# Cross-attention block on one core: layer-norm work moved within VectorE's attention step, and probability transposes that wait tile by tile

## What is computed

```python
xq = layer_norm(x, qn_w, qn_b)
ctx = layer_norm(context, cn_w, cn_b)
q = (xq @ q_w).reshape(B, N, H, D)
kv = (ctx @ kv_w).reshape(B, M, 2, H, D)
attn = jnp.einsum('bnhd,bmhd->bhnm', q, k) * scale
attn = jax.nn.softmax(jnp.where(xa_mask[:, None, :, :], neg, attn), axis=-1)
out = jnp.einsum('bhnm,bmhd->bnhd', attn, v).reshape(B, N, C) @ proj_w + proj_b
x = x + out
h = layer_norm(x, n2_w, n2_b)
return x + jax.nn.gelu(h @ fc1_w + fc1_b, approximate=False) @ fc2_w + fc2_b
```

## Time and profile before

| what | us |
|---|---|
| median of 3 runs | 1137.99 |
| lowest and highest run | 1137.99, 1138.52 |
| the profiled execution, span from first to last instruction | 1135.9 |
| TensorE busy | 1100.3 |
| VectorE busy | 606.5 |
| ScalarE busy | 404.4 |
| GpSimd busy | 234.7 |

### The profile page before, as it was taken

One profiled execution on the slowest core, in us unless ns is written; L12 is line 12 of the kernel. 1 busy time (PEld: TensorE's weight loads), 2 busy tenths in 40 slices (PEclk: granted clock), 3 DMA queues, 4 the chain that ended last, 5 costly groups with the idle time before them and its releaser, 6 DMA issues.

```text
span 1135.9 us, 16366 instructions
## 1 busy us (share of the span) xinstructions
PE 1100.3 (97%) x5849; PEld 941.0 (83%) x5849; DVE 606.5 (53%) x1154; ACT 404.4 (36%) x1158; POOL 234.7 (21%) x186
## 2 busy tenths in 40 slices
PE   4999999999999999999999999999999999999998
PEld 4789988999889888888888888888888888888887
DVE  7898999899999765632423322323333333232212
ACT  3456655566666744421211311221221131121110
POOL 2343444444554420100100100100110110010000
PEclk9999999999999999999999999999999999999999
DMA  7011111232111024202002002002001001100101
GB/s 245 8 35 58 38 38 47 65 93 65 39 57 39 29 91 145 71 19 74 1 1 75 1 2 74 1 1 74 1 1 64 13 1 38 38 1 1 38 1 38
DMA packets 40144, 48.76 MB, mean 43 GB/s; under 512 B 10965, under 2 KB 19197, under 8 KB 40087
## 3 DMA queue, kind: packets, MB, share of 16 engines
q1 hardware_dynamic: 37919, 43.74, 11.7%
q10 hardware_dynamic: 2168, 4.21, 1.0%
HBM read 30.54 MB, written 16.78 MB: 42 GB/s over the span
## 4 chain that ended last, share of the span: by engine, by line
PE 85%; DVE 5%; POOL 4%; issue 3%; ACT 2%; DMA 0%; ACTq 0%; POOLq 0%; DVEq 0%
PE bank L1304 31%; PE bank L1275 31%; PE bank L1144 7%; PE bank L1175 6%; POOL S L531 4%; PE bank L1125 4%; PE bank L1157 3%; ACT S L637 1%; PE bank L1186 1%; PE bank L1287 1%; DVE xhat L893 1%; DVE cx L773 1%; DVE esum L868 0%; PE bank L1135 0%; DVE S L828 0%
## 5 line engine op out<-in xcount | busy, mean ns | idle before, releaser
L1304 PE MATMUL bank<-w,gTh 128*128 128x512 f32 x1024 | 319.3, 393 | 0.0
L1045 DVE CAST gTh<-g 128x512 fp32r<-128x512 f32 x128 | 56.9, 444 | 442.9 <-ACT g L739 442.9
L739 ACT ACTIVATE g<-bank,cols 128x512 f32<-128x512 f32 x128 | 88.0, 688 | 471.6 <-PE bank L1275 470.1
L1304 PEld LDWEIGHTS bank<-w,gTh 128*128 128x128 f32 x1024 | 192.4, 188 | 42.7
L1304 PE MATMUL bank<-w,gTl 128*128 128x512 f32 x512 | 200.4, 391 | 0.0
L1275 PE MATMUL bank<-hT0h,w 128*128 128x512 f32 x512 | 162.2, 397 | 0.0
L1275 PE MATMUL bank<-hT1h,w 128*128 128x512 f32 x512 | 159.1, 392 | 0.1
L480 POOL TENSOR_TENSOR hrs<-hve,mhalf 128x1 f32<-128x1 f32 x32 | 17.6, 549 | 551.3 <-DVE hve L1019 551.3
L1304 PEld LDWEIGHTS bank<-w,gTl 128*128 128x128 f32 x512 | 96.1, 188 | 22.0
L1275 PEld LDWEIGHTS bank<-hT0h,w 128*128 128x128 f32 x512 | 94.7, 188 | 21.5
L1275 PEld LDWEIGHTS bank<-hT1h,w 128*128 128x128 f32 x512 | 95.1, 188 | 19.8 <-issue 0.5
(11 more groups left out here) (103 smaller groups left out, 1824.8 us busy)
## 6 DMA issues: line engine op xcount, KB each, us to landing
xr<-in_x SPq DMA_DIRECT2D x16, 512.0 KB, 3.5
x_scratch<-xr SPq DMA_DIRECT2D x16, 512.0 KB, 2.8
x<-x_scratch SPq DMA_DIRECT2D x8, 1024.0 KB, 5.6
out<-x SPq DMA_DIRECT2D x7, 1024.0 KB, 4.3
w1raw<-in_L_xattn_fc_w SPq DMA_DIRECT2D x16, 256.0 KB, 3.0
w2raw<-in_L_xattn_fc_w SPq DMA_DIRECT2D x16, 256.0 KB, 2.6
kvw<-in_L_xattn_kv_w ACTq DMA_DIRECT2D x2, 1024.0 KB, 11.1
qraw<-in_L_xattn_q_w ACTq DMA_DIRECT2D x1, 1024.0 KB, 11.6
```

The source lines that it names most:

```text
L739: act.activation(g[:, :], bF[j % 2][:, :], ACT.Gelu, bias=cols[:, F1B + j:F1B + j + 1]).then_inc(a_gelu.sem, 1)
L1045: dve.tensor_copy(gT[HI][j % 4][:, :], g[:, :]).then_inc(v_ghi.sem, 1)
L1304: mm = pe.matmul(bC[t][:, :], gT[d][j % 4][:, t * P:(t + 1) * P], w2[:, j, w, :], start=(j == 0 and i == 0), stop=(j == JT - 1 and i == 2))
```

## The change

In steps 0 to 15 (`prep` is None) VectorE executes `stats` between `masked(1, 2)` and `masked(1, 3)`, and not behind `prob_lo(3)`. It executes `variance` right behind `masked(1, 3)`, and not behind `av_lo(2)`. It executes `normed` behind `q_lo(0)`, ahead of `av_lo(1)`, and not behind `recip(0)`, ahead of `exp_sum`. GpSimd's `rstd` goes ahead of the subtraction, and stood behind it. TensorE waits for the scaling of tile 0 ahead of `prob_T1(0, 0)` and for that of tile 1 ahead of `prob_T1(0, 1)`; before, it waited for both ahead of `prob_T1(0, 0)`. No instruction that computes is added or removed, and the order in the preparation is as it was.

```diff
@@ GpSimd, step
+            def x_rstd():
+                n = k.plus(3)
+                v_veps.wait(pool, n, 0)
+                v_xhat.wait(pool, n.plus(-1), UT - 1)
+                power(rstd[:, :], veps[:, :], P).then_inc(p_rstd.sem, 1)
+
             if norm2 is not None:
                 h_rstd(static(0), norm2)
+            if norm and prep is None:
+                x_rstd()
             if scores:
                 n = k.plus(1)
                 v_max.wait(pool, n, 1)
...
-            if norm:
-                n = k.plus(3)
-                v_veps.wait(pool, n, 0)
-                v_xhat.wait(pool, n.plus(-1), UT - 1)
-                power(rstd[:, :], veps[:, :], P).then_inc(p_rstd.sem, 1)
+            if norm and prep is not None:
+                x_rstd()
@@ VectorE, step
             if scores:
                 masked(1, 2)
+            if norm and prep is None:
+                stats()
+                v_bn.wait(dve, n, UT - 1)
+            if scores:
                 masked(1, 3)
+            if norm and prep is None:
+                variance()
...
             if front:
                 q_lo(0)
+            if norm and prep is None:
+                normed()
...
-            if norm and prep is None:
-                stats()
-                v_bn.wait(dve, n, UT - 1)
             if back:
                 av_lo(2)
...
-            if norm and prep is None:
-                variance()
...
-            if norm and prep != "q":
+            if prep == "scores":
                 normed()
-            if prep == "scores":
                 values_lo(1)
@@ TensorE, prob_T1
-                if i == 0:
-                    p_prob.wait(pe, b, UT - 1)
+                if g_ == 0:
+                    p_prob.wait(pe, b, t)
```

## The result

| what | before | after |
|---|---|---|
| median of the runs, us | 1137.92 (17 runs) | 1140.09 (17 runs) |
| lowest and highest, us | 1137.13, 1138.52 | 1139.14, 1141.11 |
| span of the profiled execution, us | 1135.9 | 1138.5 |
| a loop step on TensorE, mean of steps 2 to 9, us | 23.32 | 23.43 |

The ratio is 1.002 with a 95% interval of 1.0013 to 1.0027. So the change costs about 2.2 us. That is 0.19%, right at the edge of what I had called no change. The range of 1134.5 to 1142 held it, and the direction of the small remainder is up. In all that follows, medians are of undisturbed executions; one execution, of experiment one, took 2829 us, nothing here shows why, and it is left out.

What follows compares the result with a forecast made beforehand. TensorE, busy 1100 of 1136 us, was taken to bound the kernel. A start stall of -1.40, `q(0)` +0.10 and mid-step wait +1.15 a step summed over all steps to 0.0, giving 1138.0 us, range 1134.5 to 1142.

Steps and rivals of the forecast that it cites:

- Part 1: At the step's start, TensorE's stall for GpSimd's scaling of tile 1 goes whole: 1.40 us a step.
- The new wait at `q(0)`: Near the step's start, `q(0)` waits for the second `x_lo`: 0.10 us a step, between 0 and 0.2.
- Part 2: Mid-step, early statistics and variance delay `prob_lo(2)` by 1.64 us; TensorE waits 1.15 us in each of 13 steps.
- Part 3: `normed` behind `q_lo(0)`: the pair costs 1.05 us on VectorE and TensorE loses 0, at most 0.3 a step.
- So it costs 0, with 0.05 us to spare: At `av(3)`: `prob_lo(3)` ends at 166.37 and TensorE wants it at 166.42, so no wait.
- my own sign: Prediction is wrong if `av(3)` waits for `PTl` by more than 0.1 us.
- The sum by step: Step 0 +1.15 us, steps 1 to 10 -0.15 each, 11 and 12 +0.51 each, 13 -0.6, others 0: together 0.0.
- the forecast: Whole kernel: 1138.0 us, within 0.2% of no change, a step of 23.2 to 23.3 us; chance 0.58.
- The slower one: At `av(3)`: `prob_lo(3)` is late, TensorE waits 0.25 to 0.3 us in each of 13 steps, 1141.5 us; chance 0.20.
- the change does nothing at the start: Rival: the stall at the step's start stays, +15 us, 1153 us; chance 0.02.
- the banks come free earlier: Faster rival, mid-step: the wait for `prob_lo(2)` costs 0.9 us, 13 times -0.25, 1134.8 us; chance 0.14.

Runs made afterwards that it cites:

- experiment one: Kernel before with only TensorE's wait split by tile (tile 0's scaling ahead of the first transposes, tile 1's ahead of the second): 1132.8 us, ratio 0.9956.
- nine: Changed kernel with TensorE's old wait, both scalings ahead of the first transposes: 1140.19 us, ratio 1.002.
- five: Kernel before with one edit, the normalisation right ahead of `recip(0)`, TensorE's old wait kept: 1123.3 us, ratio 0.9871.
- six: Kernel before with the normalisation ahead of `recip(0)`, plus the change's early `stats`, `variance` and `rstd`, old wait kept: 1137.64 us, ratio 1.000.
- four: Kernel before with two edits, the normalisation right ahead of `recip(0)` and TensorE's wait by tile: 1124.1 us, ratio 0.9876.
- two: Changed kernel with the normalisation put back behind `recip(0)`; early statistics, variance, `rstd` and wait by tile kept: 1147.56 us, ratio 1.0081.
- three: Changed kernel with the normalisation moved behind `prob_lo(3)`, all else as changed: 1138.12 us, ratio 0.9999.
- experiment eight: Changed kernel with the normalisation moved ahead of `q_lo(0)` instead of behind it: 1150.36 us, ratio 1.0112.

## Why the prediction was right, and where it was off

**The whole splits into three measured parts.** They come from kernels that differ in one of them, but for the wait by tile, which nine shows to be worth nothing in the changed kernel. The normalisation clear of GpSimd's scaling of tile 0: 1123.3 against 1137.9, -14.6 us (five). Statistics and variance ahead of `prob_lo(2)`: 1137.6 against 1123.3, +14.3 (six). The normalisation ahead of `prob_lo(3)` and not ahead of `recip(0)`: 1140.1 against 1137.6, +2.5 (with the old wait of TensorE on both sides, nine against six, 1140.2 against 1137.6). Together +2.2, which is the result. The wait by tile is worth 0 here (nine), and also in the fastest kernel (five against four: 0.8 us the other way, on two chips and with overlapping intervals of the ratios, so not resolved). It is worth 5 us only where the scaling of tile 1 is late (one).

**Part 1, the stall that goes: right.** I had 1.40 us a step. The timeline gives 1.32 at the first transposes and 1.38 one score later. One of my two reasons was that the pair's 3.02 us at the old place were mostly a wait for GpSimd; one swap shows it (five). The other, the wait for each tile, did nothing here (nine).

**The new wait at `q(0)`: right in kind, 0.18 and not 0.10.** I had left out that the first matmul after the wait takes 0.10 us longer (0.22 against 0.12). In part 2 I had counted some 0.1 for that as an estimate.

**Part 2, `prob_lo(2)` late: right.** I had 1.64 us of delay and 1.15 of wait; the traces have 1.65 and 1.10, and experiment six has 1.10 from medians. The rival in six, that the wait needs VectorE to be behind from elsewhere, is refuted: it is the same 0.63 in the profile's count in the changed kernel, in two, three and six.

**Part 3, the pair behind `q_lo(0)`: its price right, its consequence wrong.** I priced the pair at 1.05 us and it costs 1.03. (The 1.00 in it was the length of the merged row; to the next start an undisturbed pair takes 0.91, as in five, so the overlap with the subtraction cost 0.12 and not 0.05.) The failed step is the next one, "So it costs 0, with 0.05 us to spare". `prob_lo(3)` ends at 167.19, 0.03 ahead of the matmul's place at 167.22, as I had worked out, and TensorE is still 0.19 us late. The deadline that I used is the matmul's start. But the wait for `prob_lo(3)` also holds the weight load in front of that matmul, which goes 0.11 us ahead when nothing waits, and the load began 0.12 us after `prob_lo(3)`'s end. I had counted a hand-over and a late weight load in part 2 and neither here. By my own sign, a wait of `av(3)` by more than 0.1, this part was wrong: it is 0.19 late in starts, though the profile shows no bracket. Experiment three takes it away, and with it 2.0 us; this is most of the difference between the predicted 1138.0 and the measured 1140.1.

**The sum by step.** From the steps' starts in both traces: steps 2 to 9 cost 0.11 us more each where I had -0.15, so a step is 23.43 us and not the 23.2 to 23.3 of the forecast. Of the difference 0.19 is `av(3)`, 0.08 `q(0)`, and 0.05 that I took one step of 23.37 for all, while every other one took 23.28; 0.05 came back in part 2. Step 1 cost 0.16 more and step 10, which also holds work of the MLP block, 0.22 (23.96 against 23.74), where I had -0.15 for both. Together steps 1 to 10 took 1.3 us more and not 1.5 less. Steps 11 and 12 cost 0.3 each (I had 0.51), because the stall at their start was 0.9 in starts and not the 0.74 of the profile's count; for the same reason step 13 gained 0.97 (I had 0.64). Step 0 lost 1.26 (I had 1.15). The profiled execution after also has 0.4 us more in the preparation, whose order is unchanged. Its cause is open. Executions differ there by some of it: with the same order on VectorE, step 1 begins at 79.99 in experiment nine and at 80.23 in the changed kernel. The steps 11 to 13 came out 0.7 us better than I had them, and that hid part of the 2.8 us by which steps 1 to 10 came out worse. The time came 2.1 us above 1138.0, and the forecast's bounds were 2.3, so that it held was in part luck.

**The rivals.** The slower one named the right place, `prob_lo(3)` for `av(3)`, with "0.25 to 0.3 in each of 13 steps" and a threshold of 0.18 a step. The place and the size came true, 0.19 us. Its condition did not: the pair lost 0.12 us (1.03 to the next start, against 0.91 in experiment five) and not the whole 0.35. I gave it 0.20 and the forecast 0.58; with a room of 0.05 us against a mistake of 0.2 in the deadline, the two should have been even. That the change does nothing at the start and that the banks come free earlier are both refuted by the first timeline.

**The rule of the Trainium skill** ("SBUF — State Buffer", section "Who interferes with whom": whoever comes second stands still) fits three places. The `xhat` that met a GpSimd instruction ended 0.29 us after it in the kernel before (168.30 + 2.48, against 170.49), 0.28 after it in the changed kernel (165.08 + 0.65, against 165.45), and as much in experiment eight (167.03 + 1.43, against 168.18). GpSimd stands still in its turn: in the kernel before, its scaling was issued at 167.98, when the first `xhat` had been running since 167.84, and took 2.51 us, where it takes 2.25 elsewhere. So the price is what is left of the other's instruction and a little more, and not a property of the place in the step.

**Left open.** No run separates `stats`, `variance` and the earlier `rstd` in part 2 (`rstd` ends at 162.64 and the subtraction begins at 163.20, so it held nothing there), and the 0.18 us at `q(0)` remained in the fastest kernel.

## What to carry to other kernels

When work is moved off the end of a step, look for the release just behind its old place before looking for a new place far away: here the normalisation only had to go ahead of the reciprocals that set GpSimd going, one call earlier, and that gave 14.6 us where the longer move gave back all of it. Before moving work into the middle of a step, take the room between each producer behind it and its consumer, and compare it with the length of what is moved. Where the consumer is a matmul, the wait also holds the weight load in front of it, even if what is loaded has been ready for long. Here the producer would have had to end 0.23 us before the matmul's place (0.11 for the load ahead and 0.12 to the load's start); its 0.03 us weren't room.

## What the hardware showed that I had not expected

A wait of TensorE costs more than its length. At `q(0)` the gap is 0.08 us, and the first matmul then takes 0.22 and not 0.12. At `av(3)` the gap is 0.10 us, and the first two matmuls then take 0.33 and not 0.24. In both the weight load begins with its matmul or 0.01 us ahead of it, and not 0.11. The profile's idle column shows no bracket at `av(3)` at all, since the modelled ends of the matmuls cover it; only the distances between starts show the 0.19.
